# Merging the q/k/v projection stage of a four-layer graph transformer with the first row maxima of its attention

## What is computed

```python
h = jnp.maximum(_layernorm(x, axis=-1), 0.0)
q = (x @ W_q).reshape(Bn, Nn, NUM_HEADS, HEAD_DIM).transpose(0, 2, 1, 3)   # x here is h; k, v alike
scores = jnp.einsum('bhnd,bhmd->bhnm', q, k) / np.sqrt(HEAD_DIM).astype(np.float32)
scores = jnp.where(adj == 0, -jnp.inf, scores)
attn = jax.nn.softmax(scores, axis=-1)
out = jnp.einsum('bhnm,bhmd->bhnd', attn, v)
```

## Time and profile before

| | us |
|---|---|
| median of 3 runs (3726.48 to 3730.39) | 3727.95 |
| the profiled execution | 3729.18 |
| its span, first to last instruction | 3727.4 |
| PE, DVE, ACT, POOL busy | 3453.1, 3115.3, 1724.5, 1777.0 |
| `nodes1`: first load issued, first product, last v store issued | 689.12, 708.19, 842.91 |
| next block's first load, its first scores | 850.26, 912.55 |

### The profile page before, as it was taken

One profiled execution on the slowest core, in us unless ns is written; L12 is line 12 of the kernel. 1 busy time (PEld: TensorE's weight loads), 2 busy tenths in 40 slices (PEclk: granted clock), 3 DMA queues, 4 the chain that ended last, 5 costly groups with the idle time before them and its releaser, 6 DMA issues. The chain is left out here.

```text
span 3727.4 us, 60321 instructions
## 1 busy us (share of the span) xinstructions
PE 3453.1 (93%) x21147; PEld 1821.7 (49%) x21147; DVE 3115.3 (84%) x7052; ACT 1724.5 (46%) x3546; POOL 1777.0 (48%) x829
## 2 busy tenths in 40 slices
PE   5679999684999999999999999999997999699999
PEld 5579999550111111111111111111115999699999
DVE  6878888667999999999999999999965776477777
ACT  7811111371666666666666666666662444310100
POOL 2400000111888888888888888888891111000000
PEclk8789999895999999999999999999998999899999
DMA  6522121264011010111001110010003332211220
GB/s 237 197 98 86 52 86 58 110 233 170 5 28 28 28 29 6 28 28 28 22 13 28 28 28 10 24 30 28 5 5 104 111 114 81 111 53 52 92 81 29
DMA packets 59727, 240.72 MB, mean 65 GB/s; under 512 B 11696, under 2 KB 14128, under 8 KB 45232
## 3 DMA queue, kind: packets, MB, share of 16 engines
q1 hardware_dynamic: 59440, 236.91, 18.3%
HBM read 151.80 MB, written 85.07 MB: 64 GB/s over the span
## 5 line engine op out<-in xcount | busy, mean ns | idle before, releaser
L1366 POOL TENSOR_TENSOR a_w<-a_w,keep_mask_t 128x1024 f32<-128x1024 f32 x768 | 1631.1, 2150 | 354.2 <-ACT a_w L1351 354.2
L1351 ACT ACTIVATE a_w<-a_sc_ps 128x512 f32<-128x512 f32 x2048 | 1111.4, 595 | 780.7 <-PE a_sc_ps L1268 779.0
L1300 DVE CUSTOM_DVE_ANT_0 a_mx_ps<-a_mx_ps,a_mbias 128x512 f32<-128x512 f32 x2056 | 1353.3, 721 | 82.9 <-PE a_mx_ps L1225 70.2
L1241 PE MATMUL a_o_ps<-a_w,a_v 128*33 128x512 f32 x4096 | 1081.2, 606 | 5.9 <-POOL a_w L1366 5.8
L868 PE MATMUL g_acc<-g_hv,g_w 128*128 128x129 f32 x8192 | 922.9, 276 | 44.2 <-ACT g_hv L825 32.3
L868 PEld LDWEIGHTS g_acc<-g_hv,g_w 128*128 128x128 f32 x8192 | 921.4, 193 | 45.9 <-DVE g_w L804 45.8
L804 DVE SCALAR_TENSOR_TENSOR g_w<-g_row,keep_s,keep_mask_t 128x1024 f32<-128x1024 f32 x512 | 647.4, 1283 | 202.1 <-PE g_acc L868 185.5
L1268 PE MATMUL a_sc_ps<-a_qs,a_ks 97*128 97x512 f16 x2048 | 622.8, 386 | 0.3
L1225 PEld LDWEIGHTS a_mx_ps<-a_ks,a_qs 32*128 32x128 f16 x2056 | 92.3, 91 | 849.0 <-DVE a_mx L1300 450.7
L1313 DVE TENSOR_TENSOR a_w<-a_w,keep_mask_t 128x1024 f32<-128x1024 f32 x256 | 460.1, 1797 | 31.4 <-ACT a_w L1351 31.4
L1225 PE MATMUL a_mx_ps<-a_ks,a_qs 32*128 32x512 f16 x2056 | 396.0, 392 | 52.2 <-DVE a_mx L1300 32.7
(11 more groups left out here) (230 smaller groups left out, 2169.1 us busy)
## 6 DMA issues: line engine op xcount, KB each, us to landing
h_nodes<-p_h SPq DMA_DIRECT2D x16, 1032.0 KB, 3.9
g_h<-h_nodes SPq DMA_DIRECT2D x16, 1032.0 KB, 7.3
p_adj_in<-in_adj SPq DMA_DIRECT2D x16, 1024.0 KB, 8.3
g_row<-u_rows SPq DMA_DIRECT2D x32, 512.0 KB, 7.5
p_x<-x SPq DMA_DIRECT2D x16, 1024.0 KB, 8.8
v<-p_v SPq DMA_DIRECT2D x8, 1056.0 KB, 6.8
a_v<-v SPq DMA_DIRECT2D x16, 528.0 KB, 3.6
p_x<-in_x SPq DMA_DIRECT2D x8, 1024.0 KB, 4.9
```

The lines of the kernel that those rows point to most:

```text
L1241: mm = nc.tensor.matmul(o_ps[2 * HD * a:2 * HD * a + HD + 1, c % 2, :], v[u][:, jt, a, :], w[:, g % PB, a, :], start=(jt == 0), stop=(jt = ...
L1300: last = nc.vector.tensor_tensor_reduce(out=mx_ps[:, buf, a, :], in0=mx_ps[:, buf, a, :], in1=mbias[:, t, kc * BANK:(kc + 1) * BANK], scal ...
L1351: nc.scalar.activation(w[:, g % PB, a], sc_ps[:, n % SB], ACT.Exp, scale=SCALE).then_inc(exp_done, 1)
L1366: nc.gpsimd.tensor_tensor(w[:, g % PB], w[:, g % PB], keep["mask_t"][:, jt, c * BANK:(c + 1) * BANK].unsqueeze(1).to_broadcast([P, 2, BANK ...
```

## The change

`nodes1` and the first two chunks' maxima become one block, `nodes1_and_first_maxima`; the rest of `head_attention` becomes `heads`. A new `HeadState` holds the buffers that both use. All of it is written out for eight batches, without a loop.

- x has four buffers, which lie in the tiles 8 to 15 of `mbias`; they are normalised in place (no `hn`). `rstd` and `shift` have two buffers.
- `hi`, `lo`, `v` are rings of four quarters. SP stores each quarter as it is done: 20 DMAs a batch (128 KB each of q_hi, k_hi, q_lo, k_lo, 264 KB of v).
- `qk_ps` has three banks (four before), `v_ps` one (two before), the freed banks hold one unit of maxima, `mx_ps` (the block before had two units in turn).
- ACT copies v of even quarters, DVE of odd ones.
- The mask's tiles 0 to 7 are loaded in batches 0 and 1, 8 to 13 in batches 5 to 7, the last two at the end. The parts of q, k, v of batch 0 are loaded in batches 1 and 2.
- The 33 steps of maxima (32 units and the turn of chunk 0) go into quarters 1 to 3 of batches 2 to 7, two a quarter, one in quarter 1 of batches 2, 4 and 6.
- The fill of `ks`'s extra rows goes from DVE to POOL. `heads` starts with its main loop.

Where the units go, and where x lies:

```diff
+    units = [(0, n) for n in range(UNITS)] + [(1, n) for n in (*range(TURN), -1, *range(TURN, UNITS))]
+    quarters = (CH - 1) * (B - FIRST)
+
+    def due(b, q):
+
+        j = (CH - 1) * (b - FIRST) + q - 1
+        return range(j * len(units) // quarters, (j + 1) * len(units) // quarters) if b >= FIRST and q > 0 else range(0)
...
+        x = [hs.mbias[:, 2 * RT + 2 * k:2 * RT + 2 * k + 2, :].rearrange("p t n -> p (t n)").bitcast(F32)
+             .rearrange("p (t f) -> p t f", f=F) for k in range(RING)]
```

SP's order:

```diff
+            for b in range(B):
+                for q in range(CH):
+                    store(b, q)
+                    if b < 2:
+                        load_mbias(CH * b + q)
+                    if q == 0 and 1 <= b <= B - RING:
+                        sp.wait_ge(turned, CH * b)
+                        load(b + RING - 1)
...
+                    if q == 1 and b in (1, 2):
+                        if b == 1:
+                            for k in range(RING):
+                                sp.wait_ge(stored[k], 16 * PARTS)
+                        hs.load(sp, io, 0, b - 1)
+                        hs.load_v(sp, io, 0, b - 1)
+            sp.wait_ge(turned, CH * B)
+            for t in range(2):
+                load_mbias(T - 2 + t)
+            hs.place_shift(sp, io, 0, 0, 0)
+            for k in range(RING):
+                sp.wait_ge(stored[k], 16 * PARTS * B)
+            sp.wait_ge(hs.shift_placed, 32)
```

DVE's and PE's orders, and what `heads` no longer does:

```diff
+                for q in range(CH):
+                    split(b, q)
+                    if q == 0 and 1 <= b < B - 1:
+                        stats(b + 1)
+                    for i in due(b, q):
+                        take(i)
+                    if q == (1 if b else 0) and b + 1 < B:
+                        shifts(b + 1)
...
+                for q in range(CH):
+                    products(b, q)
+                    if q + 1 < CH:
+                        turn_nodes(b, q + 1)
+                    for i in due(b, q):
+                        score(i)
+                        break
+                    values(b, q)
+                    if q + 1 == CH and b + 1 < B:
+                        turn_nodes(b + 1, 0)
+                    for i in due(b, q)[1:]:
+                        score(i)
...
-            for chunk in range(2):
-                for k in range(SLOTS):
-                    slot(k, chunk, 0, chunk, chunk == 0)
```

More of the change, by code:

```diff
@@ L899, in nodes1 @@
+        v_kept = [s.sem(f"v_kept{g}") for g in range(2)]
+        stored = [s.sem(f"stored{k}") for k in range(RING)]
+        mx_scored, mx_taken = s.sem("mx_scored"), s.sem("mx_taken")
         block = s.block()
@@ L901, in nodes1 @@
         QK = 2 * CH
[L903 to L913, removed]
+        PARTS = 5
         @block.sync
         def _(sp):
[L917 to L944, removed]
@@ L982, in first @@
-            def first():
-                stats(0, 0, 0)
-                shifts(0)
-            def turn(b, k, i, more=True):
-                if more:
-                    stats(b + 1, 1 - k, i + k)
-                dve.wait_ge(stored[k], 80 * i)
-                split(b, k, i, 0)
-                if more:
-                    shifts(b + 1)
-                for q in range(1, CH):
-                    split(b, k, i, q)
-            dve.sem_inc(v_kept, 2)
-            dve.wait_ge(consts_ready, 3)
@@ L1030, in turn @@
-                if more:
-                    norm(b + 1, 1 - k, CH - 1)
-            act.sem_inc(hT_kept, 2)
-            turns(act, first, turn, lambda b, k, i: turn(b, k, i, False))
+                    elif b + 1 < B:
+                        keep_hT(b + 1, 0)
+                    keep_v(b, q)
+                    if q < 2 and b > 0:
+                        norm(b, q + 2)
+                    elif q >= 2 and b + 1 < B:
+                        norm(b + 1, q - 2)
         @block.tensor
@@ L1189, in _ @@
                         sp.wait_ge(scored, 2 * (BODY * b + STEPS))
-                        load(sp, b + 1, 0)
+                        hs.load(sp, io, b + 1, 0)
                     if c >= 1:
@@ L1210, in _, with slot @@
         def _(pe):
-            def slot(k, chunk, u, c, first=False):
-                n, buf = slots(first)[k], ring(k, c % 2)
-                if n < 0 and first or not wanted(n, chunk):
+            def slot(k, chunk, u, c):
+                n, buf = slots[k], ring(k, c % 2)
+                if not wanted(n, chunk):
                     return
@@ L1281, in _, with slot @@
         def _(dve):
-            def slot(k, chunk, c, parity, masks, first=False):
-                n, buf = slots(first)[k], ring(k, c % 2)
-                if n < 0 and first or not wanted(n, chunk):
+            def slot(k, chunk, c, parity):
+                n, buf = slots[k], ring(k, c % 2)
+                if not wanted(n, chunk):
                     return
```

345 lines of the change are left out of this document (218 added, 127 removed).

## The result

The changed kernel takes 3707.02 us (median of five, 3705.45 to 3712.38), the kernel before, beside it, 3727.95 (3724.62 to 3731.56): ratio 0.9945 [0.9934, 0.9956], 20.9 us less. Forecast were 3705 and 23. The profiled execution took 3706.8, its span is 3705.0, where the span before was 3727.4.

What follows compares the result with a forecast made beforehand. Bound by a ring through single buffers, the block change, then DVE alone for 41 us. Terms 28.5 + 122.9 + 3 + 12 + 4.5 + 10.3 = 181.2 against 204.4, 23.2 us less: 3705, range 3686 to 3730.

Steps and rivals of the forecast that it cites:

- read-out: At the end of a unit of maxima somebody waits for: the accumulator's read-out shows, 0.14 us, 33 times, +3 (0 to 4.6).
- Batches 0 and 1: Projection batches without maxima: statistics run a batch ahead, ACT is late next; 13.75 and 14.75, 28.5 us where 33.9 stood.
- Batches 3 to 7, quarter by quarter: Projections with maxima: DVE's units lengthen quarters; batches 3 and 5 22.4 us, 4 and 6 18.95, 7 21.25.
- The layout of one quarter: One projection quarter timed from its first product at full clock, by earlier latencies: rests done at 3.2 us, next products 3.05.
- The clock: Batches 2 to 7: PE's pauses bring the half clock, one quarter a batch at about 2 us; +12, bounds 0 and 24.
- DMA and mask: Batches 0 and 1: queued transfers exceed batch time, mask tile 7 lands late for the first unit; +4.5 us, bounds 0 and 12.
- The end: After the last quarter: last v store, two mask tiles, shift stored and placed, barrier, first scores; +10.3 us net.
- Fills on POOL: Before the first product: four fills ahead of POOL's first power reach 698.5, about when it is wanted; 0 put, to 1 us.
- Rival B: Batches 0 to 2: stores in small pieces crowd the DMA queue, about 18 us more; gain of 5, 3723; chance 0.13.
- Rival D: Batches 2 to 7: maxima don't overlap, each unit lengthens its quarter by 1.8 us; gain 13 to 14, 3715; chance 0.08.
- A: Whole stage lighter: little half clock, mask in time, read-out hidden; gain of 43, 3685; chance 0.20.
- C: Batches 2 to 7: PE stays at 1.2 GHz, 33.5 us a batch; loss of 36, 3764; chance 0.11, mixtures included.

Runs made afterwards that it cites:

- e1: The changed kernel with mask tiles 0 to 7 loaded right behind x of batch 1, instead of one tile a quarter in batches 0 and 1; 3695.82 us.
- e5: The changed kernel with each store of a quarter's q or k part made as two stores of 64 KB; 3718.46 us.

## Why the prediction was right, step by step

- Direction and total were right, and the mechanism in the main: the pairs overlap, and the quarters go as laid out. Batch 2's first wait was missed, and the total came out partly because errors cancel. The stage: 181.2 laid out, 179.6 measured. Part by part, with the read-out, clock and mask terms put where they belong: batches 0 and 1 28.5, measured 30.8; batch 2 about 26, measured 33.3; batches 3 to 7 about 116.5, measured 107.1; the end 10.3, measured 8.5. Batch 2 is 7 us over and the five behind it 9 us under: that the total came within 2 us is luck in good part.
- *Batches 0 and 1*: 28.5, measured 30.8. Batch 0's first quarter, at the half clock, took 5.8 us; 13.75 for the batch was too little for that.
- *Batches 3 to 7, quarter by quarter*: 104.0 laid out with no clock term, 107.1 measured. A quarter with no pair 3.15, as said; quarter 1 with two pairs 7.66 and 7.88, said 7.95; with one 4.34, said about 4.5; quarters 2 and 3 with two, at the full clock, 5.0 to 6.2 and 4.6 to 5.9, said 5.0 and 6.3. The layout of one quarter, from the latencies of the earlier trace rows, was the step that carried the forecast; the experiments show why it must be laid out whole, since single waits in it are worth nothing.
- *The clock*: this term was mis-sized for batches 3 to 7. Granted were 0.89 over batches 2 to 7, within the 0.75 to 0.9 named, but 0.74 of it in batch 2 and 0.94 in the five behind. Three quarters there started at the half clock (783.38, 809.96, 857.00) and cost 2.0, 1.4 and 1.7 us over their like, 5.1 instead of the 10 that five quarters at 2 would give. PE's last wait ahead of each was 2.84, 1.20 and 1.73 us; others of 2.84 (before 827.70) and 2.16 were not followed by the half clock.
- *DMA and mask*: +4.5, bounds 0 and 12, was too small. Batch 2 took 33.3 where 18.95 and 2 of clock were laid out. The mask wait that I named is there (4.88), but later, and ahead of it is one that I left out: PE waits 6.54 for the parts, with values and products queued behind. I had the 24 us of transfers for a 14.75 us batch in my hand, and let the ring of four quarters swallow the delay; the ring covers stores up to its depth, and the parts have no ring. They are read back from what batch 0's stores write, and stand behind them in the queue. I also counted bytes and not SP's issues, which fill SP from 717 to 767. e1 gave 11.2 us back in batch 2 alone.
- *The end*: batch 7 and the end were 21.25 + 10.3 = 31.6, measured 30.9 (857.00 to 887.87), of which 3.9 is the shift's store behind the mask. The place and the size were right.
- *Fills on POOL*: four take 7.37 us and the first power starts at 698.30, as said (698.5); the first product moved by 0.1.
- *Rival B*: its sign, casts or rests that wait for `stored`, does not show in after. Nor does e5 show a stage bound by stores: its 10.5 us stand where SP's issues come late, in batch 2 and at the end, and batches 3 to 7 take what they took. In batch 2 of after, 739 to 760, 4381 packets with 6.91 MB moved at 329 GB/s, 3458 of them under 2 KB. By that row the Trainium skill's rule for transfers under 1 MiB ("DMA: Bandwidth & Descriptors", section Bandwidth), which pointed to 3723, gives too high a price for a mix of mostly 128 KB stores and loads here.
- *Rival D* measured alone: 3725.8, not the 3715 that I gave it. I had priced a pair at 1.8 us; behind the projections, at the half clock, it is 2.11, which over 33 steps is the 10 us. D as a mechanism, that the pairs lengthen their quarters by all they cost, is refuted by 179.6 for 202.0.
- *A and C*: neither; the clock was between them as forecast, nearer to A from batch 3 on. Of the signs, batch 3 was within 22 to 27 us (23.9), batch 5 below (20.4), and the wait for the mask ended at 760 and not at 751.

## What to carry to other kernels

When transfers of a stage exceed its time for a batch or two, ask of each queued transfer who waits for it first: a ring hides late stores up to its depth (without pairs ACT waited 6.6 us for one), but not a load that stands behind them, and moving bulk loads that nobody wants yet into an idle stretch of the queue was worth 11 us here. Count the issues as well as the bytes: at 0.47 us each they filled SP, and doubling those of q and k cost 10 us. Place extra work of one engine by the order on that engine, not by the other engines' gaps: the quarter that looked emptiest on PE was a bad one for a pair, since DVE had its statistics there and the half clock followed. And before a single hand-over in a circle of three engines is shortened, lay out the whole circle: two such edits moved waits from one engine to the next and no time.

## What the runs showed of the hardware

SP issued a DMA in 0.43 to 0.48 us as a rule. Single ones took far longer: 2.89 and 1.29 us in batch 2 with the DMA share at 1.03, but also 1.54 at 862.94 with the share at 0.46, and 2.21 in e1 with 0.28, so a full queue is not what sets it, and the cause is open. Each makes everything behind it on SP late. The 12 parts of 128 KB took a median of 7.9 to 8.8 us from issue to landing in after, 3.3 to 3.8 in e1 and 4.4 to 5.3 in e5, with the DMA share at 1.05, 0.99 and 1.07: the share does not tell how late a transfer will be. What also remains open is the clock: pauses of 1.2 to 2.8 us on PE were followed by the half clock in three quarters of after and in other quarters of its sister kernels, others as long were not, and no row here tells which pause will be.
